# Two stacked graph layers with window LSTMs on one core: the even tokens of the p = 1 step are written by VectorE instead of ScalarE

## The reference

```
h = relu(layernorm(x));  x = x + L0(h, adj)
h = relu(layernorm(x));  x = x + L1(h, adj)

L0:  h = relu(adj @ (h @ Wg0 + bg0));  h = relu(adj @ (h @ Wg1 + bg1))
     for p in 1..4:                          # one LSTM with its own weights for each p
         wins = h[:, :T//p*p].reshape(B * (T//p), p, 128)
         last = last hidden state of the LSTM over the p tokens of each window
         h[:, p-1::p] = last                 # the window's last token is replaced
L1:  agg = A_hat @ h;  h = relu(batchnorm(agg @ W1.T + b1));  out = batchnorm(h @ W2.T + b2)
```

## Time and profile before

| | |
|---|---|
| median of 3 runs | 617.47 us (616.46 to 617.72) |
| the profiled execution | 617.47 us, its span 615.7 us |
| PE matmul busy | 525.0 us, 85% |
| DVE busy | 445.2 us, 72% |
| ACT busy | 335.0 us, 54% |
| POOL busy | 170.2 us, 28% |
| L591, the copy of the even tokens, on ACT | 16 times, 10.7 us |
| L850, L852 on DVE | 16 times each, 11.1 and 6.9 us |

### The profile page before, as it was taken

How to read it: one execution, slowest core, us unless ns; L and a number is a source line. 1 busy time by engine, 2 the same in 40 slices (tenths; PEclk the granted TensorE clock), 3 DMA queues, 4 the chain that set the end, 5 groups by cost and what they waited for, 6 DMA issues and landing times.

```text
span 615.7 us, 8124 instructions
## 1 busy us (share of the span) xinstructions
PE 525.0 (85%) x2769; PEld 447.2 (73%) x2769; DVE 445.2 (72%) x1049; ACT 335.0 (54%) x636; POOL 170.2 (28%) x276
## 2 busy tenths in 40 slices
PE   4579899798989898999999999999698978766646
PEld 3467768687978687988876888997487877544436
DVE  3264466888875888878678887875778887557766
ACT  2433575454437755655586566557756655245654
POOL 2341003201030263125005430500141020809951
PEclk9679999999889999999999999999999999697997
DMA  7200002000000110201021101012710000500007
GB/s 224 67 2 35 2 0 86 18 18 1 17 2 35 52 52 35 69 2 68 2 86 51 36 36 51 3 50 102 275 34 1 19 17 12 195 0 1 0 0 274
DMA packets 17837, 31.21 MB, mean 51 GB/s; under 512 B 1498, under 2 KB 6020, under 8 KB 17796
## 3 DMA queue, kind: packets, MB, share of 16 engines
q1 hardware_dynamic: 17092, 30.30, 14.2%
q10 hardware_dynamic: 704, 0.39, 0.2%
HBM read 19.16 MB, written 11.53 MB: 50 GB/s over the span
## 4 chain that ended last, share of the span: by engine, by line
issue 66%; POOL 18%; POOLq 7%; PE 4%; DVE 3%; ACT 1%; DVEq 0%
POOL x_pre L328 6%; POOLq L326 5%; POOL y_post L328 5%; POOL z_back L370 5%; POOLq L324 2%; PE gate_ps L961 1%; POOL z_ring L370 1%; PE gate_ps L963 1%; PE gate_ps L962 1%; PE gate_ps L1168 1%; DVE x_back L953 1%; POOL ln_post L323 1%; POOL ln_pre L323 1%; DVE stats L757 0%; DVE hid_lo L652 0%
## 5 line engine op out<-in xcount | busy, mean ns | idle before, releaser
L577 ACT ACTIVATE gate<-gate_ps,gate_bias 128x256 f32<-128x256 f32 (+2 forms) x312 | 160.4, 565 | 30.4 <-PE gate_ps L963 28.8
L582 ACT ACTIVATE gate<-cell 128x512 f32<-128x512 f32 (+2 forms) x88 | 45.3, 515 | 123.1 <-DVE cell L832 74.4
L961 PE MATMUL gate_ps<-by_class_hi,wih_hi 128*128 128x256 f32 (+2 forms) x264 | 86.6, 328 | 11.8 <-issue 10.9
L963 PE MATMUL gate_ps<-by_class_lo,wih_hi 128*128 128x256 f32 (+2 forms) x264 | 84.6, 320 | 0.0
L962 PE MATMUL gate_ps<-by_class_hi,wih_lo 128*128 128x256 f32 (+2 forms) x264 | 84.4, 320 | 0.0
L961 PEld LDWEIGHTS gate_ps<-by_class_hi,wih_hi 128*128 128x128 f32 x264 | 50.9, 193 | 19.8 <-issue 13.7
L322 POOL TENSOR_TENSOR ln_post<-mv_post,eps 128x4 f32<-128x4 f32 x16 | 5.3, 333 | 203.2 <-DVE mv_post L698 203.2
L961 PE MATMUL gate_ps<-hstep_hi,whh_hi 128*128 128x256 f32 (+2 forms) x192 | 60.9, 317 | 0.0
L962 PE MATMUL gate_ps<-hstep_hi,whh_lo 128*128 128x256 f32 (+2 forms) x192 | 60.8, 316 | 0.0
L963 PE MATMUL gate_ps<-hstep_lo,whh_hi 128*128 128x256 f32 (+2 forms) x192 | 60.6, 316 | 0.0
L322 POOL TENSOR_TENSOR ln_pre<-mv_pre,eps 128x4 f32<-128x4 f32 x16 | 4.6, 288 | 194.8 <-DVE mv_pre L698 194.8
(11 more groups left out here) (247 smaller groups left out, 1396.8 us busy)
## 6 DMA issues: line engine op xcount, KB each, us to landing
x_pre<-in_x SPq DMA_DIRECT2D x16, 256.0 KB, 2.7
x<-in_x SPq DMA_DIRECT2D x16, 256.0 KB, 2.7
z_spill<-z_ring SPq DMA_DIRECT2D x8, 512.0 KB, 2.7
z_back<-z_spill SPq DMA_DIRECT2D x8, 512.0 KB, 7.2
x_spill<-x SPq DMA_DIRECT2D x12, 256.0 KB, 2.0
x_back<-x_spill SPq DMA_DIRECT2D x1, 3072.0 KB, 11.4
out<-x_back SPq DMA_DIRECT2D x12, 256.0 KB, 2.1
x<-in_adj SPq DMA_DIRECT2D x1, 1024.0 KB, 6.4
```

The source lines that it names most:

```text
L577: nc.scalar.activation(gate[:, tile_of(g), gt, 0:size], gate_ps[k % GATE_BANKS][:, 0:size], ACT.Tanh if gt == G_GATE else ACT.Sigmoid, bia ...
L582: nc.scalar.activation(gate[:, tile_of(g), G_GATE, 0:size], cell[:, tile_of(g), 0:size], ACT.Tanh)\
L961: nc.tensor.matmul(ps, w[0], m[0], start=start, stop=False)
L963: return nc.tensor.matmul(ps, w[0], m[1], start=False, stop=stop)
```

## The change

The copy on ACT is gone. DVE computes the even tokens a second time, o tanh(c) for every second token straight from the two gate buffers, and writes the product into `h32`; it does so behind the low part of the class split, and in rounds 1 to 3 it waits for `turn_mm` there. The gate buffers are read longer, so ACT waits for `even_done` of turn g before it overwrites gate G in turn g+2. The `cell` buffer is no longer read by ACT after `h_done`, so DVE's wait for `even_done` ahead of the next cell is gone. `T // 2` columns are read as the first half of the gate buffers, as the copy read the first half of `cell`: the tokens of this layer lie even ones first, then odd ones.

```diff
@@ scalar, lstm_turn
                         if gt == G_GATE:
                             act.wait_ge(h_done, prev + 1)
+                            act.wait_ge(even_done, FIRST_BEFORE[prev + 1])
@@ scalar
-            def even_tokens(g):
-
-                r, chain, p, step, sub, nb = TURNS[g]
-                act.wait_ge(h_done, g + 1)
-                if r > 0:
-                    act.wait_ge(turn_mm, batch_of(r - 1, chain, sub) + 1)
-                nc.scalar.activation(h32[:, chain, 0::2, sub], cell[:, tile_of(g), 0:T // 2], ACT.Copy)\
-                    .then_inc(even_done, 1)
-
             for slot in range(N_SLOTS):
                 lstm_turn(slot)
                 for splits in (True, False):
-                    if not splits and TURNS[slot][2] == 1:
-                        even_tokens(slot)
                     for kind, n in PRE_AFTER[slot]:
@@ vector, lstm_turn
                 else:
-                    if PREV[g] is not None and TURNS[PREV[g]][2] == 1:
-                        dve.wait_ge(even_done, FIRST_BEFORE[PREV[g] + 1])
                     dve.wait_ge(gates_act, k + 2)
                     nc.vector.tensor_tensor(c_, i_, g_, ALU.mult).then_inc(cell_ready, 1)
@@ vector, lstm_turn, p == 1
                     nc.vector.tensor_copy(hi, c_).then_inc(class_hi, 1)
                     dve.wait_ge(class_hi, CLASS_AT[r, chain, 1, sub])
                     low(lo, c_, hi).then_inc(class_lo, 1)
+                    if r > 0:
+                        dve.wait_ge(turn_mm, batch_of(r - 1, chain, sub) + 1)
+                    nc.vector.tensor_tensor(h32[:, chain, 0::2, sub], gate[:, tile_of(g), O_GATE, 0:T // 2],
+                                            gate[:, tile_of(g), G_GATE, 0:T // 2], ALU.mult).then_inc(even_done, 1)
```

## The result

The changed kernel takes 621.51 us (median of 9 runs, 618.79 to 624.54) against 617.47 in the same comparison. The ratio is 1.0073, interval 1.0052 to 1.0094: 3.2 to 5.8 us slower, 4.5 at its centre. Forecast were 623.7, range 620.3 to 626.4. Its nine runs spread over almost 6 us, the nine of before here over under 2; but 35 runs of the kernel before in a later comparison spread over 4.5 (615.1 to 619.6), so the spread by itself says little.

The account below looks back on a forecast made before the run. DVE's line, for which PE waits in the p=1 turns, was taken as the bound. Rounds 0 to 3 add 0.46 + 1.80 + 1.80 + 2.13 = 6.2 us to 617.5, giving 623.7, range 620.3 to 626.4.

Parts of the forecast that it names:

- The place: In the p=1 turns opening each round PE waits for DVE; an instruction added ahead delays PE and the end fully.
- The count of 11: Over rounds 0 to 3, the new instruction's 0.60 us reaches PE 11 times, less 0.41.
- The price: New strided DVE multiplication lasts 0.68 us and takes 0.60 from DVE's line; low end 0.34, high end 0.69.
- ACT's relief, 0.41: ACT's removed copies let its gates start earlier: 0.14 us gained in round 0, 0.27 in round 3.
- The slack of 0.70 ahead of turn 23: DVE's gap before L837 of turn 23, held by ACT's gates, hides turn 22's 0.60 us with 0.10 left.
- The new waits: DVE's wait for turn_mm and ACT's wait for even_done at gate G two turns later cost nothing.
- The packed price as a rival (620.8): DVE's strided write costs only L859's packed price, 0.34 us in line: 620.8 us; chance 0.20.
- The clock as a rival (625.4): PE's round 3 stall grows from 2.83 to 3.4 us, then 3.4 us at half clock lose 1.7: 625.4; chance 0.18.
- Hidden: PE's p=1 stalls have another cause, DVE's instruction fills idle time, only 0.41 relief remains: 617.1 us; chance 0.07.
- faster by ACT's relief: In round 3 PE's stalls are for gate banks ACT frees; three shrink by 0.76 each: 614.8 us; chance 0.05.

Follow-up runs that it names:

- e2: Changed kernel with DVE's even-token multiplication moved behind the pre-chain's low part and the residual sum; 620.05 us, ratio 1.0061 to the kernel before.
- e1: Changed kernel with DVE's even-token multiplication moved into the next turn's wait for tanh, both new waits kept; 615.28 us, ratio 0.9983 to the kernel before.
- e3: Changed kernel with the multiplication writing packed floats into a spare buffer in rounds 1 to 3; 619.93 us, ratio 1.0057 to the kernel before.
- e5: Changed kernel with even tokens written in round 0 only, by nobody in rounds 1 to 3; 616.38 us, ratio 0.9994 to the kernel before.
- e6: Kernel before, ACT still copying, with only DVE's wait for turn_mm added in rounds 1 to 3; 616.42 us, ratio 1.0003.
- e4: Changed kernel with a second, packed multiplication of 256 columns right ahead of the new one; 625.73 us, ratio 1.0157 to the kernel before.
- e7: Kernel before with the even tokens copied from the cell buffer by POOL instead of ACT; 616.85 us, ratio 1.0002.
- e8: Kernel before with POOL copying the even tokens and the residual sum L749 moved into the next turn's tanh gap; 615.05 us, ratio 0.9966.
- e10: Kernel before with round 3's residual sum in its own turn's tanh gap; even tokens by DVE's tanh gap, by POOL in round 3; 612.37 us, ratio 0.9937.
- e9: Kernel before, ACT still copying, with the residual sum moved into its own turn's tanh gap in round 3 only; 616.42 us, ratio 0.9993.

## Why the prediction was right, step by step

- **The place.** PE's stalls in the p=1 turns are where DVE's line comes through: right. All three of rounds 1 and 2 grew, and in round 3 the three for L749 and the one for hstep; later stalls hardly took it back (1.58 and 0.34 us later in round 1 are 1.57 and 0.34). The last transposes come at 529.03 instead of 524.28. e2 shows that the position in DVE's line doesn't matter, e1 that only its idle time does.
- **The count of 11.** 11 x 0.445 - 0.41 = 4.49; the stalls add up to 4.48. Right.
- **The price.** This is the mis-sized term. The duration was put at 0.68 and measured 0.61, and "0.68 - 0.09" assumed that a strided instruction overlaps with the next as a packed one does. It overlaps by 0.16, so 0.445 goes into the line, not 0.60; half of the difference is duration, half is overlap. 11 x 0.155 = 1.7 of the 2.2 us between 623.7 and 621.5; by the ratio, 4.5 us, nothing more is missing. The stride does cost, as e3 shows with nothing but the destination changed: 0.19 us of duration, less than the 0.25 taken over from ACT's rows. Those compare a copy with a tanh, and L766, the other row, also reads at the stride. The Trainium skill (Advanced Engine Details and Errata, Memory Cachelines) says that SBUF accesses need at least two hits on a line of 16 bytes and pay otherwise; e3 agrees for the write, and the page has no size.
- **ACT's relief, 0.41.** Right, within 0.1: in round 0 0.13 by e1 (1.15 to 1.02), 0.14 forecast; in round 3 0.36 by e5, and 0.27 by e1 without the 0.13 of its `hstep_lo`, 0.27 forecast. The rest of the 10.7 us was worth nothing.
- **The slack of 0.70 ahead of turn 23 hides one.** Right: from h to the next cell 3.85 us, 3.83 before.
- **The new waits cost nothing.** Right: e6 for turn_mm, and e1 keeps both.
- **The packed price as a rival (620.8).** Wrong: the duration is 0.61, not 0.43. e3, with the packed price in rounds 1 to 3, shows what it would be: +3.4 us of stalls. The same place at the packed price still costs three quarters of the time.
- **The clock as a rival (625.4).** Its event happened in the profiled run; whether it is the change's doing isn't settled. The stretch behind the first hstep of round 3 had the clock at 1.2 GHz behind stalls of 3.28, 3.19, 3.16 and 3.60 us (changed, e2, e3, e4), but also behind 2.70 (e1) and 2.81 (e7), and stayed at 2.4 GHz behind 2.79, 2.83 and 2.83 (e5, e6, before). Where it is the only fall up to the tail (e2, e3, e4, e7), hstep to the tail takes 1.5 to 1.6 us longer; in e1, where it lasted from 446 to 451, 2.9. Nor does it need so long a stall: in e8 the clock fell behind one of 2.16 us, in e10 behind 2.54. The mean granted clock on record for each run says a little about how often: it is below 0.955 in 10 of the changed kernel's 19 runs and in all 5 of e4, but in 7 of 69 of the kernel before. So a lower clock comes more often with the longer stalls. Its price isn't clear from this: the ten runs average 622.3 us and the nine others 621.0, but in e9, no slower than before, 7 of 11 are below 0.955. The stalls alone give the measured 4.5 us.
- **Hidden, or faster by ACT's relief.** The first is excluded by the time itself, the second by e5: with nobody writing the even tokens in rounds 1 to 3 the time is that of before, so there was no gain of 2 us waiting on ACT. e9 and e10 show when it would be there: once DVE's line is shorter.

Windows just behind the first hstep of round 3, of e7 (stall 2.81):

```profile
444.00:447.30 3.30, 3.30 (x8) 2.62 (x9) 2.54 (x5) 1.63 (x3) 2.07 (x3) 0.51 0.09 11
```

and of e6 (stall 2.83):

```profile
446.30:449.60 3.30, 3.30 (x15) 2.73 (x16) 2.53 (x5) 1.76 (x4) 2.14 (x3) 1.00 0.02 7
```

## What to carry to other kernels

Busy shares don't say where an engine has room: DVE at 72% had none in these turns, and its only gap lay inside them, in the wait for another engine. Before work is moved, look for the gaps of the receiving engine at that place; the same instruction cost 4.5 us in line and nothing in the gap. Price it by how much later the next instruction starts, not by its duration. Where two engines' lines through a loop are equally long, relieving one shows nothing until the other is relieved too, so a null result of one edit is no verdict on the pair.

## What was not expected of the hardware

- What a DVE instruction takes from its engine's line isn't its duration: with 256 columns at a step of 16 bytes it lasts 0.61 us and the next starts after 0.45; packed 0.42 and 0.33; with 512 packed columns 0.69 and 0.60. The overlap is 0.09 for packed ones and 0.16 for the strided one.
- The strided write costs DVE 0.19 us over the same instruction with a packed destination (e3). ACT's strided copy lasts 0.25 longer than its packed tanh of 256 columns (672 and 418 ns); a packed copy on ACT wasn't run.
- Beside a strided copy on POOL (1.3 us for 256 columns) a DVE instruction lasts 0.76 instead of 0.69 us. Beside POOL's `y_post` `hstep_lo` lasts 0.82, 0.74 or 0.69, by when POOL's instruction starts.
- Stalls of PE of equal length (2.79 to 2.83 us) were followed by the full clock in three profiles and by half of it in one, at the same place of the same work, and shorter ones (2.16 in e8, 2.54 in e10) by half of it too.
